# Thirty-six transposes of the identity matrix that nothing reads, on TensorE between the first position transposes and the first tokens

## The reference

```python
x = x + tanh(g_xattn[0]) * xattn(layernorm(x), ctx, ...)
x = x + tanh(g_ffn[0]) * ffn(layernorm(x), w_gate, w_up, w_down)

def xattn(x, pos, ...):
    emb = x + pos
    q, k, v = emb @ wq + bq, emb @ wk + bk, emb @ wv + bv
    w = pos_bias * (abs(i - j) < 64)
    ek, ew = exp(k - max_over_tokens(k)), exp(w - max_over_rows(w))
    y = sigmoid(q) * (ew @ (ek * v)) / (ew @ ek)
    a = layer_norm(y @ wo + bo + emb) * gamma + beta
    return layer_norm(relu(a @ w1 + b1) @ w2 + b2 + a) * gamma + beta

def ffn(x, ...):          # activations rounded to 8 bits per token, weights to -1, 0, 1 times a scale
    return bitlinear(silu(bitlinear(x, w_gate)) * bitlinear(x, w_up), w_down)
```

## Time and profile before

| | |
|---|---|
| median of three runs | 529.32 us (527.03 to 531.65) |
| profiled execution | 531.71 us, span 530.0 us |
| PE busy | 478.4 us, 90% |
| DVE busy | 432.7 us, 82% |
| ACT busy | 372.8 us, 70% |
| POOL busy | 245.8 us, 46% |
| mean granted TensorE clock | 0.965 |

### The profile page before, as it was taken

The page is one execution under the profiler, slowest core; times in us unless marked ns, Lnnn a source line. Parts: engine busy times, 40 slices in busy tenths (PEclk is TensorE's granted clock), DMA queues, the critical chain, the costliest instruction groups (busy, mean ns, idle before and its releaser), DMA issues. The chain is left out here.

```text
span 530.0 us, 9499 instructions
## 1 busy us (share of the span) xinstructions
PE 478.4 (90%) x2912; PEld 390.5 (74%) x2912; DVE 432.7 (82%) x992; ACT 372.8 (70%) x594; POOL 245.8 (46%) x386
## 2 busy tenths in 40 slices
PE   0499579999999999999999999999999999897394
PEld 0389468998887888779877888788778987775132
DVE  3676985958798989898989898998899789768474
ACT  2467874556868957886788769787768776886563
POOL 2863016318712575354743484348415903574410
PEclk9997998999999999999999999999999999999577
DMA  5965142101301233023302331222123202232301
GB/s 175 276 205 179 28 69 64 41 0 41 80 22 21 61 90 91 16 54 91 90 12 40 80 92 51 40 62 76 44 41 81 61 0 39 61 71 52 79 0 41
DMA packets 69328, 36.01 MB, mean 68 GB/s; under 512 B 47008, under 2 KB 68768, under 8 KB 69280
## 3 DMA queue, kind: packets, MB, share of 16 engines
q1 hardware_dynamic: 68160, 35.14, 26.1%
q10 hardware_dynamic: 1120, 0.27, 0.2%
HBM read 20.46 MB, written 4.19 MB: 47 GB/s over the span
## 5 line engine op out<-in xcount | busy, mean ns | idle before, releaser
L530 POOL TENSOR_TENSOR mv<-mv,cols 128x2 f32<-128x2 f32 x64 | 12.5, 195 | 176.6 <-DVE mv L1558 176.6
L2444 PE MATMUL ps<-w_hi,h_hi 128*128 128x256 f32 x256 | 75.8, 296 | 0.0
L2444 PE MATMUL ps<-w_lo,h_hi 128*128 128x256 f32 x256 | 71.6, 280 | 0.0
L2444 PE MATMUL ps<-w_hi,h_lo 128*128 128x256 f32 x256 | 71.5, 279 | 0.0
L907 ACT ACTIVATE h_hi<-ps,cols 128x512 fp32r<-128x512 f32 x64 | 43.8, 685 | 19.8 <-PE ps L2444 15.5
L1611 DVE RECIPROCAL ps<-ps 128x512 f32<-128x512 f32 x16 | 53.6, 3355 | 0.6 <-PE ps L2518 0.6
L2444 PE MATMUL ps<-n1T_hi,w_hi 128*128 128x512 f32 x128 | 51.3, 401 | 0.8 <-DVE n1T_lo L1640 0.8
L2444 PE MATMUL ps<-n1T_lo,w_hi 128*128 128x512 f32 x128 | 50.6, 396 | 0.0
L2444 PE MATMUL ps<-n1T_hi,w_lo 128*128 128x512 f32 x128 | 50.6, 395 | 0.0
L2444 PEld LDWEIGHTS ps<-w_hi,h_hi 128*128 128x128 f32 x256 | 48.3, 189 | 2.8 <-DVE h_lo L1646 0.2
L2444 PEld LDWEIGHTS ps<-w_lo,h_hi 128*128 128x128 f32 x256 | 48.3, 188 | 1.1
(11 more groups left out here) (175 smaller groups left out, 1460.9 us busy)
## 6 DMA issues: line engine op xcount, KB each, us to landing
emb<-in_ctx_dram SPq DMA_DIRECT2D x16, 256.0 KB, 3.1
x_in<-in_x_dram SPq DMA_DIRECT2D x16, 256.0 KB, 2.9
work<-in_x_dram SPq DMA_DIRECT2D x8, 512.0 KB, 3.9
out_dram<-work SPq DMA_DIRECT2D x16, 256.0 KB, 2.1
work<-in_L_xattn_w_dram SPq DMA_DIRECT2D x2, 1024.0 KB, 8.4
work<-in_L_ffn_w_gate_dram SPq DMA_DIRECT2D x1, 1024.0 KB, 5.6
work<-in_L_ffn_w_up_dram SPq DMA_DIRECT2D x1, 1024.0 KB, 5.6
place_c<-in_L_ffn_w_down_dram SPq DMA_DIRECT2D x1, 1024.0 KB, 4.9
```

Of the source, the lines that this page charges most:

```text
L530: pool.tensor_tensor(mv[:, n, c, 1], mv[:, n, c, 1], eps_col[:, c], ALU.add).then_inc(power_step[n].sem, 1)
L2444: last = nc.tensor.matmul(dst, lhsT, rhs, start=(i == 0 and not begun), stop=(i == n - 1 and ends))
```

## The change

A function is added that issues 36 transposes of the identity into the first 128 columns of bank 7, and it is called once, behind `positions_T(0)`. It has no wait and raises no semaphore. Nothing else differs.

```diff
+WARM_UP = 36
...
+            def warm_up():
+                for _ in range(WARM_UP):
+                    nc.tensor.transpose(ps[:, 7, 0:P], ident[:], ident[:])
...
             pe.wait_ge(const_ok, 5)
             pe.wait_ge(dve_const_ok, 5)
             positions_T(0)
+            warm_up()
             emb_rows(0, 0)
             emb_rows(0, 1)
             keys_T(0, 0)
```

## The result

The changed kernel takes 526.23 us (median of 20 runs, 523.52 to 528.79), the kernel before 529.67 us (20 runs in the same sessions, 527.03 to 532.79): ratio 0.9924, 95% interval 0.9906 to 0.9942. That is 3.4 us faster, 0.65% by the medians and 0.76% by the ratio: within the 1% that was called no change, and inside the forecast range, but more than five times the forecast gain of 0.6 us. The profiled execution has a span of 524.4 us, 5.6 less than before; this pair lies further apart than the medians.

A forecast was written before the change was run, and what follows sets the result against it. TensorE was taken to bound the long middle, not the front fill stage; of 3.5 us saved there 2.9 became wait, leaving -0.6 us: 528.7 us against the median 529.32, range 525.3 to 532.3.

The forecast's parts named there:

- Same within 1%: Whole kernel: time between 524.0 and 534.6 us, not told from no change; chance 0.89.
- The transposes' own time: PE's idle time from 12.2 to 19.4 us hides the 36 transposes; cost 0 to 0.7 us of delay of emb_rows.
- Transposes lift the clock: Front of PE: f32 transposes raise its clock from 1.2 to 2.4 GHz, spacing falling from 0.22 to about 0.11 us.
- rival 1: Front: transposes don't lift the clock and only occupy PE until 20.1 us; +0.5 us, 529.8; chance 0.15.
- What the fast clock gives: Front: 3.5 us of PE time saved from emb_rows through keys_values, 2.9 lost in waits, 0.6 us left.
- Rival 2: Front: clock lifted, then lost in a new idle gap of about 24.6 to 26.95 us; +1.7 us, 531.0; chance 0.20.
- Nobody waits for these transposes; only PE's own queue stands behind them: Transposes in the front: no other engine is held by them, only PE's later work; no size of its own.
- the transfers counted as none added: Transposes in the front: the edit moves nothing and adds no transfer; no cost counted.
- Rival 4: PE's slow stretches at 38.4 to 45.0 and 79.4 to 82.6 us vanish or multiply; -4.7 to +3 us; chance 0.13.

The follow-up runs named there:

- early36: Against the kernel before: the same 36 transposes, but placed ahead of `positions_T(0)`; 526.52 us, ratio 0.9939.
- onecol: Changed kernel with its 36 transposes replaced by 18 one-column f32 identity products (36 instructions on PE) in the same place; 525.88 us, ratio 0.9921 to the kernel before.
- again36: The changed kernel run once more, unaltered, for a second profile; 526.75 us, ratio 0.9944 to the kernel before.
- shift256: Kernel before plus 128 one-column f16 products (256 PE instructions) around `positions_T(0)`, no transposes; 529.29 us, ratio 0.9996.
- shift128: Kernel before plus 64 one-column f16 products (128 PE instructions) ahead of `positions_T(0)`, no transposes; 527.37 us, ratio 0.9964.
- late72: Kernel before plus 36 one-column f16 products (72 PE instructions) ahead of `attend(1, num, 1, 2)`, behind 77 us; 527.54 us, ratio 0.9978.
- hold: Changed kernel plus 8 transposes behind `emb_rows(0, 1)` and 16 behind `keys_values(0, 0)`, filling idle gaps; 525.97 us, ratio 0.9923 to the kernel before.
- w36shift256: Changed kernel plus 92 one-column f16 products ahead of `positions_T(0)`, 256 PE instructions more than before in all; 528.16 us, ratio 0.9980 to the kernel before.

## Why the prediction was right or wrong

**The range held the time, and the forecast's reason didn't.** "Same within 1%" came true; 526.2 lies inside 525.3 to 532.3. The forecast of -0.6 us from the clock in the front is a size that no run here can tell from zero, and the measured -3.4 us is something else. That the range held it is luck: the range was made for the spread and the rivals, and this cause is in none of them.

*The transposes' own time: right.* They start at 12.23 and end before the tokens, 6.16 us in all, hidden.

*Transposes lift the clock: right, rival 1 is out.* 36 in 6.16 us, eight token transposes in 1.09 and 1.04 us, and in early36 a stretch at 0.50 from 11.4 us, which a clock that never rose could not show. The Trainium skill's sentence (TensorE: Matmul & The Clock Gate, part 4) that transpose-mode work doesn't count as busy doesn't hold for these f32 transposes, which the trace records as plain MATMUL; whether they run in the mode that the page means, no row says. The one-column products of onecol, equally dense, did not lift it.

*What the fast clock gives: the step failed in its place.* I let `keys_T` start 0.9 us sooner and put the new gap ahead of `keys_values(0, 1)`. But `keys_T(0, 0)` writes bank 0, which holds the transposed tokens until embT_lo is made, and embT_lo stands in DVE's order behind the statistics of x_in. I had followed that kind of wait for `keys_values` and not for `keys_T`. PE waited 2.79 and 1.71 us there, in the two profiles, and `keys_T` started at 23.76 and 21.57 us; 0.9 us sooner would have been 21.2. In again36 the rest went as the sum has it: a short wait of 0.85 us for the second maximum, then everything at 0.235 us a product. Over the runs the early clock can't be seen in DVE's bias: it starts between 30.20 and 30.67 us in onecol, shift256, shift128 and late72, without the lift, and at 30.48 in hold and w36shift256, with it.

*Rival 2 (lifted and lost again): it happened, in the profiled execution,* at the gap ahead of `keys_T`: 23.4 to 30.0 us at 0.50. That DVE's bias is 1.65 us late, against a priced 1.7, is chance: the slow clock cost nothing against before, and the 1.65 us are those by which `keys_T` began later, for want of x_in. Nor does it decide the median: hold, which bridges the gaps, is no faster than the change beyond the noise.

*The step that failed for the result: "Nobody waits for these transposes; only PE's own queue stands behind them", and the transfers counted as none added.* Instructions are themselves transferred. 72 more move every later border of PE's instruction packets, and in the kernel before three of those packets met data that the chain waits for: 1.1 us each at the up weights, at emb of batch 6 and at the tokens of batch 5, by the table of the places. Sum 3.3 us in the first profile, 2.1 to 3.3 in the five with 72 or 120 more in the front, whose medians gain 2.9 to 3.7; about 0.7 us on the average is not accounted for. That the whole hangs on the number of instructions and their place and not on the clock ahead of the tokens, onecol and early36 show, and shift256 against both. What each single place is worth I have from profiles alone; late72, made to part them, agrees, but its interval reaches to no change.

*Rival 4 (later slow stretches move) is at most a small part of the gain, and much of the spread.* The fall behind 38 us lasts 6.8 us in the three profiles of before, 3.4 us in those of the change and again36, and is missing in onecol, shift256 and shift128; executions of one kernel differ by it and by the front, up to 4 us at DVE's first reciprocal (51.77 and 47.81 us in the two profiles of the change). It isn't what the edit does, for shift256 lacks it in its profile and is no faster by its median. The one at 79.4 us cost 1.5 us in the profile of before, by the step from -0.62 to -2.16 in the table. It was there in one of three profiles of before and in none of the ten others: as an estimate, a third of 1.5, 0.5 us of the mean. Whether the packet brings it about is open, since two profiles of before have the gap of 2.3 to 2.4 us and not the fall. Open is also how often the meetings between 388 and 421 us take part of the gain back; and no run moves the first packet alone, so that it is worth 1.1 us by itself isn't shown.

## What to carry to other kernels

An edit that adds instructions to an engine which runs a long unrolled program also moves the transfers of its instructions. Before a gain or a loss under 1% is put down to what the edit does, run a control with as many instructions that do nothing, and one with a whole packet's worth (256 here), which brought most of the borders back, if not the one at the up weights. To find the places, look for transfers on the chain that are longer than their like, and for a packet of kind "instruction" inside them. For a clock that is to be up at a certain point, look at every wait between the lift and the use, those for PSUM banks too.

## What the runs showed of the hardware

PE's instructions come while the program runs, in packets of 16 KB, 25 for 6441 instructions and 26 for 6697. One such packet takes 0.9 to 1.8 us on its DMA engine, and a transposing transfer with one among its packets stood nearly still for 1.2 us: 5.49 us from issue to use instead of 4.38 at the up weights, landing after 4.3 us instead of 3.0 at the hidden rows (again36). A two-part load of 0.52 MB with one inside, at 370.5 us, landed 4.6 us after its issue instead of 2.8 (GpSimd's wait 2.32 instead of 0.54 us). The clock column of these traces says 1.00 ahead of its first change, also where products stand 0.42 us apart and the clock is at 1.2 GHz; the spacing of like matmuls is what tells there. A PE gap of 1.7 us kept the full clock, one of 2.79 us lost it, gaps of 2.3 to 2.4 us did either, and one of 3.0 us kept it.
